# A typed graph layer: bf16 thirds of x replaced by two float32r parts, and a count matrix built and multiplied in two halves

## The chip, the cores and the metric

One Trainium2 chip, one core used. The metric is the device time of one launch in microseconds (us); lower is better. TensorE (PE) multiplies matrices into PSUM, VectorE (DVE) and ScalarE (ACT) work on tensors in SBUF and PSUM, GpSimd (POOL) here issues the indirect transfers that gather rows, SyncE (SP) issues most other transfers.

## The reference, cut to what matters

```python
N, E, D = 12500, 400000, 128            # nodes, edges (sorted by dst), features
def layer(X, src, dst, edge_types, W_data, b_data, W_control, b_control, W_self, b_self):
    Xs = X[src]
    m_data = Xs @ W_data.T + b_data
    m_ctrl = Xs @ W_control.T + b_control
    msg = where((edge_types == 0)[:, None], m_data, m_ctrl)
    agg = segment_sum(msg, dst, num_segments=N)
    return relu(agg + (X @ W_self.T + b_self))
result = layernorm(x + layer(x, ...))   # over the last axis, eps 1e-5, all float32
```

Since the weights come after a sum, the kernel first sums the x rows of each node's incoming edges, once for each of the two edge types, and multiplies the two sums by the two weights afterwards.

## The kernel before, in words

The nodes are split in two parts that are worked on at the same time.

**By matrix (dense blocks).** The first 88 x 64 = 5632 destination nodes are taken in blocks of 64 nodes. For a block the kernel needs a matrix of counts: for each source node (98 chunks of 128) and each of 128 columns (64 nodes x 2 types) how many edges there are. The edges of a node are looked at as up to 64 keys. A *batch* is 8 columns' worth of work in each half of the partitions: VectorE writes one-hot matrices `hot_p` (source node within its chunk) and `hot_q` (chunk and type) by comparing tables with keys (`make_onehots`, L1126), TensorE multiplies them (`build`, L634: 8 matmuls of 196 columns, in two PSUM buffers z = 0 and 1), and ScalarE moves each buffer into `cnt` (`evacuate`, L848, two copies of 784 elements). The one-hots of two groups of 64 partitions are multiplied in different row halves of the array. Eight batches make a block. Then `apply` (L652) multiplies the block's counts by x: 98 matmuls accumulated in `apply_ps`, with one 128x128 chunk of `cnt` as the stationary operand and the matching chunk of `x3` as the moving one. `x3` holds x as three bf16 parts side by side and a column of ones, 385 columns, so that the bf16 products add up to the exact float32 sum. VectorE adds up the three parts (`post`), TensorE turns the result, ScalarE takes it to `fin`.

**By gather.** The edges from tile 1395 on (tiles of 128 edges) are taken in 173 rounds of 10 tiles. For each tile GpSimd issues an indirect transfer of 128 rows into `rows`. A matmul with a one-hot matrix of 64 columns (`hot`, made by `make_hot`) adds them up in `sum_ps` (`gather_sums`, L616; even and odd tiles write different halves of the PSUM partitions). The first 12 rounds gather float32 rows of x, and ScalarE takes the sums (`take_sums`). All later rounds gather bf16 rows of 768 bytes from `x3_dram`, which ScalarE's queue wrote at the start, and VectorE adds up the parts (`add_parts`, L1188). A moving window of sums in `acc` is updated by `add_sums`.

**Order.** The whole program is a list of steps written out by the same Python loop for each engine. In step s TensorE does, in this order: `gather_sums` if a round starts here, `build(s)`, the step's one job in the PSUM tile `misc` (transposes, products with the weights), then one eighth of `apply` (12 or 13 matmuls). The apply of a block runs 8 steps behind its build; `cnt` has two buffers, one per block. There are 88 x 8 = 704 batches and so some 712 steps. A gather round starts every fourth step (a few places are left out), and GpSimd's ten transfers of a round wait at three places for `built` (`QUARTER`, L45), so that they spread over four steps.

The handshake that matters below: `build(n)` writes buffer z only when ScalarE has emptied it of batch n-1:

```python
                    if j >= 2:
                        pe.wait_ge(evacuated, j - 1)
...
                for z in range(2):
                    act.wait_ge(built, 2 * n + z + 1)
```

Before the steps, x is loaded in 14 chunks and split (`split_hi` and `split_mid` on ScalarE, `split_rest` and `split_low` on VectorE). The keys are written to DRAM in 11 pieces from which GpSimd gathers each block's keys.

Of the kernel before, what the change touches and what calls it, by code (L numbers as in the profile page):

```python
# [8 lines left out]
F32 = mybir.dt.float32  # L9
BF16 = mybir.dt.bfloat16  # L10
# [6 lines left out]
P = 128  # L17
D = 128
GT = 5
WIN = 32  # L20
TYPE_STEP = 16384
# [4 lines left out]
BLOCKS = 88  # L26
DENSE = BLOCK * BLOCKS
GATHER_0 = 1395
# [5 lines left out]
KEY_TILES = 1441  # L34
EW = 64
SLOTS = 20
F32_ROUNDS = 12
ROW = 3 * D
AHEAD = 2
BUILD_AT = 0  # L40
APPLY_AT = BUILD_AT + 8
XB = 7
FIRST_X = 5
DKCH = 11
# [5 lines left out]
def gnn_resnorm(nc, x, src, dst, etype, w_data, b_data, w_ctrl, b_ctrl, w_self, b_self, out):  # L50
# [8 lines left out]
    XBLOCKS = -(-N // P)  # L59
    XCH = XBLOCKS // XB  # L60
# [4 lines left out]
    assert KEY_TILES % DKCH == 0 and SLOTS == AHEAD * 2 * GT  # L65

    places = (BATCHES + APPLY_AT) // 4 - (0 if BLOCKS == 86 else 1)
    spare = places - PAIRS
    left_out = {2 * ((places * (2 * i + 1) // (2 * spare)) // 2) + 1 for i in range(spare)}
    gather_step = [4 * j for j in range(places) if j not in left_out][:PAIRS]  # L70
    assert len(gather_step) == PAIRS
# [95 lines left out]
    with ctx:  # L167
        def sb(name, shape, dt=F32):
            return ctx.enter_context(nc.sbuf_tensor(name, shape, dt))

        def sem(name):
            return ctx.enter_context(nc.semaphore(name))
# [6 lines left out]
        x3_dram = nc.dram_tensor("x3_dram", [N, ROW], BF16).ap()  # L179
# [11 lines left out]
        key_t = sb("key_t", [P, GROUPS * GT])  # L191
        off_i = sb("off_i", [1, GROUPS], I32)
# [27 lines left out]
        out_sb = sb("out_sb", [P, 2, D])  # L220
# [7 lines left out]
        key_ok = sb("key_ok", [P, 2, EW])  # L228
# [14 lines left out]
        xs = [cnt[:, 1, 14 * i:14 * i + 14, :].rearrange("p b c -> p (b c)").bitcast(F32) for i in range(3)]  # L243
# [12 lines left out]
        def region(b0, nb, dt):  # L256
            return x3[:, b0:b0 + nb, :].rearrange("p b c -> p (b c)").bitcast(dt)
# [1135 lines left out]
```

## Time and profile before

| | us |
|---|---|
| median of 3 runs | 2812.58 (2806.29 to 2814.47) |
| the profiled execution, its own time | 2784.88 |
| its span, first to last instruction | 2783.0 |
| TensorE busy with matmuls | 2364.6 (85%) |
| GpSimd / VectorE / ScalarE busy | 1691.7 / 1266.1 / 1224.5 |

"Busy" counts the time in which at least one instruction of that kind runs. A matmul's duration contains the time to drain the array, so consecutive matmuls overlap: their spacing, not their duration, is what a stream costs. The granted TensorE clock was 0.96 of full speed on average.

### The profile page before, as it was taken

How to read it: one execution, taken by the hardware profiler on the slowest of the kernel's cores; microseconds unless marked ns; L12 is line 12 of the kernel's file. 1: busy time of each engine (PE TensorE's matmuls, PEld its weight loads, DVE VectorE, ACT ScalarE, POOL GpSimd, SP SyncE). 2: the span in 40 equal slices, each digit the busy share in tenths (PEclk: the TensorE clock that was granted, in tenths of full speed). 3: DMA queues.
4: the chain of work that ended last, by engine and by line, in shares of the span. 5: the costliest groups of instructions: out<-in, count | busy, mean ns of one | idle time of the engine just before them, and what ended most of it. 6: DMA issues, size and time to landing. Idle time of an engine off the chain costs nothing.

```text
span 2783.0 us, 47819 instructions
## 1 busy us (share of the span) xinstructions
PE 2364.6 (85%) x17776; PEld 1301.3 (47%) x17776; DVE 1266.1 (45%) x4037; ACT 1224.5 (44%) x1997; POOL 1691.7 (61%) x1785
## 2 busy tenths in 40 slices
PE   3688888888888888888889888988888888888988
PEld 2344444544444444444445454444444444444444
DVE  8444444445444444444444454444444444444443
ACT  6344444444444444444444444444444444444443
POOL 6466665666666665666666666566666666656662
PEclk9899999999999999999999999999999999999999
DMA  7712222222222222222222222222222222222221
GB/s 191 223 47 67 71 72 59 73 68 74 72 73 71 73 72 62 74 69 75 71 72 73 69 75 71 63 69 73 74 69 73 71 73 72 69 61 72 71 75 34
DMA packets 150380, 211.42 MB, mean 76 GB/s; under 512 B 35298, under 2 KB 120725, under 8 KB 150147
## 3 DMA queue, kind: packets, MB, share of 16 engines
q0 software_dynamic: 83232, 170.57, 22.0%
q1 hardware_dynamic: 54177, 28.15, 3.7%
q10 hardware_dynamic: 12738, 9.60, 1.1%
q8 instruction: 145, 2.38, 0.3%
q14 instruction: 88, 0.72, 0.1%
HBM read 189.78 MB, written 18.41 MB: 75 GB/s over the span
## 4 chain that ended last, share of the span: by engine, by line
PE 44%; another core or an unknown queue 23%; ACT 14%; DVE 9%; issue 7%; DVEq 2%; DMA 1%; SPq 0%; ACTq 0%
PE apply_ps L664 25%; ACT cnt L860 13%; PE build L648 8%; PE sum_ps L630 4%; DVEq L1177 2%; DVE hot_q L1136 2%; DVE hot_p L1136 1%; PE misc L673 1%; DVE acc L1183 1%; PE misc L714 1%; DVE sg L1193 1%; PE misc L717 1%; DMA key_dram<-fin 1%; PE misc L692 1%
## 5 line engine op out<-in xcount | busy, mean ns | idle before, releaser
L560 POOL DMA_INDIRECT rows<-x_dram,src_t x1610 | 1524.7, 947 | 947.5 <-issue 383.4
L860 ACT ACTIVATE cnt<-build 128x784 bf16<-128x784 f32 x1408 | 1087.5, 822 | 1457.1 <-remote 773.1
L664 PE MATMUL apply_ps<-x,cnt 128*128 128x385 bf16 x8624 | 1611.2, 337 | 31.0 <-issue 25.5
L664 PEld LDWEIGHTS apply_ps<-x,cnt 128*128 128x128 bf16 x8624 | 868.3, 103 | 604.7 <-issue 135.7
L648 PE MATMUL build<-hot_q,hot_p 64*128 64x196 bf16 x5632 | 425.1, 254 | 274.2 <-ACT cnt L860 205.6
L648 PEld LDWEIGHTS build<-hot_q,hot_p 64*128 64x128 bf16 x5632 | 197.6, 95 | 572.7 <-issue 372.7
L1136 DVE TENSOR_TENSOR hot_q<-const_ps,key_pq 128x784 bf16<-128x784 bf16 x704 | 390.3, 554 | 0.0
L1181 DVE TENSOR_TENSOR acc_deg<-misc,acc_deg 2x32 f32 x346 | 61.9, 179 | 671.2 <-remote 278.7
L1136 DVE TENSOR_TENSOR hot_p<-const_ps,key_pq 128x512 bf16<-128x512 bf16 x704 | 291.2, 414 | 43.1 <-DVE acc L1183 16.5
L560 POOL DMA_INDIRECT rows<-in_x,src_t x120 | 122.8, 1024 | 76.8 <-issue 30.5
L1191 DVE TENSOR_TENSOR zg<-t_mask,sum_ps 128x2 f16<-128x2 f32 x161 | 24.9, 154 | 307.5 <-PE sum_ps L630 158.3
L630 PE MATMUL sum_ps<-rows,hot 128*64 128x385 bf16 x1610 | 162.5, 331 | 0.0
L1216 DVE SCALAR_TENSOR_TENSOR y_sb<-misc,x_u 128x128 f32<-128x128 f32 (+3 forms) x105 | 30.4, 290 | 268.1 <-PE misc L717 163.9
L1041 DVE TENSOR_TENSOR hot<-const_ps,key_t 128x640 bf16<-128x640 f32 (+1 forms) x173 | 140.9, 814 | 0.0
L630 PEld LDWEIGHTS sum_ps<-rows,hot 128*64 128x64 bf16 x1610 | 77.1, 108 | 76.7 <-issue 52.1
L1193 DVE TENSOR_REDUCE sg<-sum_ps 128x128 f32<-128x384 f32 x161 | 88.7, 551 | 0.0
L1183 DVE TENSOR_TENSOR acc<-misc,acc 128x64 f32 x346 | 77.7, 225 | 2.1 <-issue 2.1
L1210 DVE TENSOR_TENSOR zd<-t_mask,apply_ps 128x2 f16<-128x2 f32 x88 | 13.6, 155 | 127.2 <-remote 45.6
L673 PE MATMUL misc<-ident,sg 128*128 128x128 f32 x173 | 58.8, 340 | 0.0
L692 PE MATMUL misc<-ident,x_u 128*128 128x128 f32 (+3 forms) x105 | 35.0, 333 | 27.1 <-DVEq L1186 14.3
L672 PE MATMUL misc<-picks,zg 128*2 128x64 f16 x173 | 33.2, 192 | 25.9 <-DVEq L1099 19.4
L537 POOL DMA_INDIRECT key_raw<-key_dram,key_at x44 | 41.8, 949 | 21.5 <-issue 13.1
(182 smaller groups left out, 1082.5 us busy)
## 6 DMA issues: line engine op xcount, KB each, us to landing
rows<-x_dram,src_t POOLq DMA_INDIRECT x1610
x_dram<-x ACTq DMA_DIRECT2D x13, 672.0 KB
cnt<-in_x SPq DMA_DIRECT2D x13, 448.0 KB
x_u<-in_x SPq DMA_DIRECT2D x43, 64.0 KB
out<-out_sb SPq DMA_DIRECT2D x43, 64.0 KB
key_dram<-fin SPq DMA_DIRECT2D x12, 196.5 KB
x_u<-in_x SPq DMA_DIRECT2D x40, 53.5 KB
out<-out_sb SPq DMA_DIRECT2D x40, 53.5 KB
```

Source lines behind the costliest of these rows:

```text
L560: pool.indirect_dma_start(out=rows_f[:, slot, 0:D] if early else rows[:, slot, 0:ROW], out_offset=None, in_=x if early else x3_dram, in_of ...
L630: last = pe.matmul(sum_ps[part, 0:ROW + 1], hot_b[:, ps % 3, st, :], rows[:, slot, 0:ROW + 1], start=(j == 0), stop=(j == GT - 1))
L648: last = pe.matmul(build_ps[z][:, o:o + 2 * XBLOCKS], hot_p[half, slot, :, i], hot_q[half, slot, :, i], start=True, stop=True)
L664: last = pe.matmul(apply_ps[:, 0:385], cnt[:, k % 2, b, :], x3[:, b, 0:385], start=(b == 0), stop=(b == XBLOCKS - 1))
L673: pe.transpose(misc[:, 0:P], sg[:, ps % 2, 0:D], ident[:, :]).then_inc(misc_full, 1)
L692: pe.transpose(misc[:, 0:v.r], x_u[0:v.r, i % 3, :], ident[0:v.r, 0:v.r]).then_inc(misc_full, 1)
L860: act.activation(o, i.rearrange("p h (m b) -> p b h m", b=XBLOCKS), ACT.Copy).then_inc(evacuated, 1)
L1041: dve.tensor_tensor(to[:, ps % 3, :, :], const_ps[:, HOT].unsqueeze(1).to_broadcast([P, 2 * GT, 2 * WIN]), keys.unsqueeze(2).to_broadcast( ...
L1136: last = dve.tensor_tensor(to[:, z:z + 2, :, :], table.unsqueeze(1).to_broadcast([P, 2, w, 2]), keys.unsqueeze(2).to_broadcast([P, 2, w, 2 ...
L1181: dve.tensor_tensor(dw, misc[0:2, P + 32 * g:P + 32 * g + 32], dw, ALU.add)
L1183: dve.tensor_tensor(aw, misc[:, 64 * g:64 * g + 64].rearrange("p (t w) -> p t w", t=2), aw, ALU.add).then_inc(acc_step, 1)
L1193: dve.tensor_reduce(sg[:, ps % 2, 0:D], sum_ps[:, 0:ROW].rearrange("p (k d) -> p d k", k=3), AX.X, ALU.add).then_inc(sg_ready, 1)
```

## The change

1. **x in two parts.** `x2` holds x as two float32r parts (a high part and the rest) and two columns of ones, 258 columns. The moving operand and `cnt` both become float32r. The split needs one ScalarE pass and one VectorE pass per chunk in place of two and two. `post` adds two parts.
2. **Two halves of source blocks.** `cnt` has two buffers of 49 chunks each (a half, in 4 bytes an element) in place of two of 98 (in 2 bytes). A batch now covers 16 columns in each half of the partitions for 49 of the 98 chunks: `build` is 16 matmuls of 98 columns. Four batches make a half, eight a block as before. `hot_p` is made once per two halves (1024 elements every other group of four batches), `hot_q` keeps 784 elements a batch. `evacuate` still moves 2 x 784 elements, now as float32r.
3. **Apply** runs by halves, 4 steps behind, in portions of 6, 12, 12, 12 and 7 matmuls; the last 7 stand at the start of the step in which the next half begins.
4. **98 blocks by matrix** instead of 88: 784 batches, 9604 apply matmuls; 157 gather rounds in place of 173, one every 5.02 steps.
5. **All gathers are float32** rows of 512 bytes from x itself, with float32 matmuls of 129 columns. `x3_dram`, its writes and `add_parts` are gone; ScalarE's `take_sums` (two short instructions) serves all rounds.
6. Smaller: `key_t` and the comparison table in bf16 with the type as a half step, `hot` in two buffers, `hot_q` for three batches instead of four, dense keys in 15 pieces, outputs normalised in place (`out_sb` is gone), loads of x without waiting for the split up to chunk 6, small tensors put over other ones.

```diff
-BLOCKS = 88
+BLOCKS = 98
-GATHER_0 = 1395
+GATHER_0 = 1555
-ROW = 3 * D
+ROW = 2 * D
-APPLY_AT = BUILD_AT + 8
+APPLY_AT = BUILD_AT + 4
+PORTIONS = (6, 12, 12, 12, 7)
-DKCH = 11
+DKCH = 15
...
+    gather_step = [(BATCHES + APPLY_AT) * r // PAIRS for r in range(PAIRS)]
...
-        x3 = sb("x3", [P, XBLOCKS, 386], BF16)
-        cnt = sb("cnt", [P, 2, XBLOCKS, P], BF16)
+        x2 = sb("x2", [P, XBLOCKS, ROW + 2], F32R)
+        cnt = sb("cnt", [P, 2, HALF, P], F32R)
-        rows = sb("rows", [P, SLOTS, ROW + 2], BF16)
-        hot = sb("hot", [P, 3, 2 * GT, 2 * WIN])
-        hot_p = sb("hot_p", [P, 8, P, 2], BF16)
-        hot_q = sb("hot_q", [P, 8, 2 * XBLOCKS, 2], BF16)
+        rows = sb("rows", [P, SLOTS, D + 1])
+        hot = sb("hot", [P, 2, 2 * GT, 2 * WIN])
+        hot_p = sb("hot_p", [P, 16, P, 2], BF16)
+        hot_q = sb("hot_q", [P, 12, 2 * HALF, 2], BF16)
...
             def build(n):
...
-                    for i in range(2):
-                        slot = (2 * n + z) % 8
+                    for j in range(4 * z, 4 * z + 4):
+                        pair, r = divmod(j, 2)
                         for h in range(2):
-                            half = slice(64 * h, 64 * h + 64)
-                            o = WIDE * h + 2 * XBLOCKS * i
-                            last = pe.matmul(build_ps[z][:, o:o + 2 * XBLOCKS], hot_p[half, slot, :, i],
-                                             hot_q[half, slot, :, i], start=True, stop=True)
+                            part = slice(64 * h, 64 * h + 64)
+                            o = WIDE * h + 2 * HALF * (j % 4)
+                            last = pe.matmul(build_ps[z][:, o:o + 2 * HALF], hot_p[part, 4 * q4 + pair, :, r],
+                                             hot_q[part, 4 * (n % 3) + pair, :, r], start=True, stop=True)
                     last.then_inc(built, 1)
...
-                for b in range(b0, b1):
-                    last = pe.matmul(apply_ps[:, 0:385], cnt[:, k % 2, b, :], x3[:, b, 0:385],
+                for i in range(b0, b1):
+                    b = half * HALF + i
+                    last = pe.matmul(apply_ps[:, 0:ROW + 2], cnt[:, half, i, :], x2[:, b, :],
                                      start=(b == 0), stop=(b == XBLOCKS - 1))
...
             for s in range(STEPS):
+                y, c = divmod(s - APPLY_AT, 4)
+                if c == 0 and 0 < y <= 2 * BLOCKS:
+                    apply(y - 1, 4)
                 if s in gather_at:
                     gather_sums(gather_at[s])
                 if batch_at(s) is not None:
                     build(batch_at(s))
...
-                if F32_ROUNDS <= gather_at.get(s, 0):
-                    add_parts(gather_at[s])
...
-                if gather_at.get(s, PAIRS) < F32_ROUNDS:
+                if s in gather_at:
                     take_sums(gather_at[s])
...
                 for z in range(2):
                     act.wait_ge(built, 2 * n + z + 1)
-                    c0 = 8 * (2 * (n % 8) + z)
-                    o = cnt[:, k % 2, :, c0:c0 + 8].rearrange("p b (h m) -> p b h m", h=2)
-                    i = build_ps[z][:, :].rearrange("p (h c) -> p h c", h=2)[:, :, 0:4 * XBLOCKS]
-                    act.activation(o, i.rearrange("p h (m b) -> p b h m", b=XBLOCKS), ACT.Copy
+                    c0 = 32 * q4 + 16 * z
+                    o = cnt[:, y % 2, :, c0:c0 + 16].rearrange("p b (h m) -> p b h m", h=2)
+                    i = build_ps[z][:, :].rearrange("p (h c) -> p h c", h=2)[:, :, 0:8 * HALF]
+                    act.activation(o, i.rearrange("p h (m b) -> p b h m", b=HALF), ACT.Copy
                                    ).then_inc(evacuated, 1)
```

How the rows stand on TensorE in the steady part, first in the kernel before, four steps that contain one gather round (L630). Each row is a run of equal instructions, its output tile, its inputs, the output's shape and the count:

```order
L673 MATMUL misc<-ident,sg 128x128
L664 MATMUL apply_ps<-x,cnt 128x385 x12
L648 MATMUL build<-hot_q,hot_p 128x196 x8
L678 MATMUL misc<-picks,zd 2x64
L679 MATMUL misc<-ident,sd 128x128
L664 MATMUL apply_ps<-x,cnt 128x385 x12
L648 MATMUL build<-hot_q,hot_p 128x196 x8
L692 MATMUL misc<-ident,x_u 128x106
L664 MATMUL apply_ps<-x,cnt 128x385 x13
L630 MATMUL sum_ps<-rows,hot 64x385 x10
L648 MATMUL build<-hot_q,hot_p 128x196 x8
```

The same engine in the changed kernel (L638 is `build`, L656 `apply`, L620 `gather_sums`):

```order
L665 MATMUL misc<-ident,sg 128x128
L656 MATMUL apply_ps<-x,cnt 128x258 x12
L638 MATMUL build<-hot_q,hot_p 128x98 x16
L670 MATMUL misc<-picks,zd 2x64
L671 MATMUL misc<-ident,sd 128x128
L656 MATMUL apply_ps<-x,cnt 128x258 x19
L638 MATMUL build<-hot_q,hot_p 128x98 x16
L656 MATMUL apply_ps<-x,cnt 128x258 x6
L638 MATMUL build<-hot_q,hot_p 128x98 x16
L656 MATMUL apply_ps<-x,cnt 128x258 x12
L620 MATMUL sum_ps<-rows,hot 64x129 x10
```

Between two builds there were always 12 or 13 apply matmuls; now there are 12, 12, 19 (12 and the 7 left over) and 6 in turn. Each float32 matmul of L620 is written here once, and shows as two instructions in a trace.

On ScalarE, a stretch of the changed kernel (L833 is `evacuate`, L816 and L818 `take_sums`, L862 the normalising, L850 and L856 the copy of x and the square root):

```order
L856 ACTIVATE std<-mv,eps_t 128x1
L816 ACTIVATE sg<-sum_ps 128x129
L818 ACTIVATE zg<-t_mask,sg 128x2
L833 ACTIVATE cnt<-build 128x49x16 x4
L856 ACTIVATE std<-mv,eps_t 107x1
L862 ACTIVATE y_sb<-y_sb,shift,rstd 128x128
L833 ACTIVATE cnt<-build 128x49x16 x2
```

The pair L816 and L818 stands ahead of the two copies of its step, in every round; before, it stood there in the first 12 rounds alone, and VectorE did that work in the others.

## Rows read from the trace of the kernel before

**Rows 1.** The page: TensorE's busy time, and its granted clock in 40 slices.
```profile
PE 2364.6 (85%) x17776; PEld 1301.3 (47%) x17776; DVE 1266.1 (45%) x4037; ACT 1224.5 (44%) x1997; POOL 1691.7 (61%) x1785
PEclk9899999999999999999999999999999999999999
```

**Rows 2.** Busy time of each engine by stretch, the start and one steady stretch.
```profile
core 0: us, PE busy (x) PEld busy (x) DVE busy (x) ACT busy (x) POOL busy (x), PEclk, DMA share, GB/s
0.00:40.00 40.00, 12.14 (x67) 9.68 (x67) 31.90 (x101) 18.68 (x27) 23.99 (x29) 1.00 0.86 226
40.00:100.00 60.00, 27.45 (x197) 14.65 (x199) 41.70 (x111) 33.42 (x48) 35.82 (x35) 0.89 0.75 225
1200.00:1600.00 400.00, 349.36 (x2597) 189.91 (x2598) 179.58 (x573) 175.55 (x285) 253.66 (x268) 0.95 0.26 72
```

**Rows 3.** The page's costliest groups: count, busy us, mean ns, idle before.
```profile
L560 POOL DMA_INDIRECT rows<-x_dram,src_t x1610 | 1524.7, 947 | 947.5 <-issue 383.4
L860 ACT ACTIVATE cnt<-build 128x784 bf16<-128x784 f32 x1408 | 1087.5, 822 | 1457.1 <-remote 773.1
L664 PE MATMUL apply_ps<-x,cnt 128*128 128x385 bf16 x8624 | 1611.2, 337 | 31.0 <-issue 25.5
L648 PE MATMUL build<-hot_q,hot_p 64*128 64x196 bf16 x5632 | 425.1, 254 | 274.2 <-ACT cnt L860 205.6
L1136 DVE TENSOR_TENSOR hot_q<-const_ps,key_pq 128x784 bf16<-128x784 bf16 x704 | 390.3, 554 | 0.0
L1136 DVE TENSOR_TENSOR hot_p<-const_ps,key_pq 128x512 bf16<-128x512 bf16 x704 | 291.2, 414 | 43.1 <-DVE acc L1183 16.5
```

**Rows 4.** Groups by shape, window 0 to 150: the builds done by then.
```profile
L648 PE MATMUL build<-hot_q,hot_p 64*128 64x196 bf16 x185 | 17.6, 294 | 34.5 <-ACT cnt L860 21.9 <-DVE hot_q L1136 7.3 <-issue 4.3
```

**Rows 5.** Timeline: a stretch of 12 apply matmuls, and one of 49.
```profile
1402.19 2.14 PE L664 MATMUL apply_ps<-x,cnt 128*128 128x385 bf16 x12
...
2761.21 8.25 PE L664 MATMUL apply_ps<-x,cnt 128*128 128x385 bf16 x49
```

**Rows 6.** Timeline: float32 products with the weights, back to back.
```profile
1405.04 0.39 PE L715 MATMUL misc<-w_t,fin 128*128 128x128 f32 x2
...
1405.27 0.39 PE L716 MATMUL misc<-w_t,fin 128*128 128x128 f32 x2
```

**Rows 7.** Timeline: a float32 gather round and a bf16 one on TensorE.
```profile
138.29 1.32 PE L627 MATMUL sum_ps<-rows,hot 128*64 128x129 f32 x20
...
1407.95 1.01 PE L630 MATMUL sum_ps<-rows,hot 128*64 128x385 bf16 x10
```

**Rows 8.** Timeline: half a batch of build, and two whole ones.
```profile
1400.14 0.35 PE L648 MATMUL build<-hot_q,hot_p 64*128 64x196 bf16 x4
...
1387.22 0.53 PE L648 MATMUL build<-hot_q,hot_p 64*128 64x196 bf16 x8
...
1404.26 0.52 PE L648 MATMUL build<-hot_q,hot_p 64*128 64x196 bf16 x8
```

**Rows 9.** Timeline: ScalarE's copies of the two whole batches of rows 8.
```profile
1387.62 0.82 ACT L860 ACTIVATE cnt<-build 128x784 bf16<-128x784 f32 x1 [0.90 <-issue]
...
1407.39 1.54 ACT L860 ACTIVATE cnt<-build 128x784 bf16<-128x784 f32 x2 [4.08 <-remote]
```

**Rows 10.** Timeline: two consecutive gathers on GpSimd.
```profile
1402.67 0.94 POOL L560 DMA_INDIRECT rows<-x_dram,src_t  x1 [0.30 <-issue]
...
1403.92 0.95 POOL L560 DMA_INDIRECT rows<-x_dram,src_t  x1 [0.31 <-issue]
```

**Rows 11.** Timeline: ScalarE's part of an early float32 round.
```profile
141.62 0.28 ACT L843 ACTIVATE sg<-sum_ps 128x129 f32<-128x129 f32 x1 [4.26 <-remote]
141.94 0.29 ACT L845 ACTIVATE zg<-t_mask,sg 128x2 f16<-128x2 f32 x1
```

**Rows 12.** Groups by shape, window 0 to 150: a copy that writes float32 with a stride.
```profile
L803 ACT ACTIVATE key_t<-build 128x512 f32<-128x512 f32 x2 | 2.2, 1124 | 0.0
```

**Rows 13.** The lines of build: durations ns min/median/max, first and last start us.
```profile
L648 PE MATMUL build<-hot_q,hot_p x5632: 243/246/364, 37.4 to 2746.4; 64*128 64x196 bf16 x195
```

More of the change, by code:

```diff
@@ L9 @@
 F32 = mybir.dt.float32
+F32R = mybir.dt.float32r
 BF16 = mybir.dt.bfloat16
@@ L20 @@
 WIN = 32
-TYPE_STEP = 16384
 EPS = 1e-5
@@ L64, in gnn_resnorm @@
     assert (TILES - GATHER_0) % (2 * GT) == 0 and BLOCKS % 2 == 0 and XBLOCKS % XB == 0 and DENSE > WIN_0
[L65 to L71, printed above, removed]
+    assert KEY_TILES % DKCH == 0 and SLOTS == AHEAD * 2 * GT and sum(PORTIONS) == HALF
+    gather_step = [(BATCHES + APPLY_AT) * r // PAIRS for r in range(PAIRS)]
     taken = set()
@@ L169, in sb, with under @@
             return ctx.enter_context(nc.sbuf_tensor(name, shape, dt))
+        def under(name, shape):
+            with nc.sbuf_tensor(name, shape, F32) as t:
+                return t
         def sem(name):
@@ L463, in _ @@
                     load_dkeys(c + 2)
+            sp.wait_ge(dkeys_written, 16 * (DKCH + 1))
+            for i in range(3):
+                load_unit(i, units[i].n0, units[i].r)
             for s in range(STEPS):
@@ L625, in gather_sums @@
                     part, st = slice(64 * g, 64 * g + 64), g * GT + j
-                    if ps < F32_ROUNDS:
-                        last = pe.matmul(sum_ps[part, 0:D + 1], hot[:, ps % 3, st, :], rows_f[:, slot, 0:D + 1],
-                                         start=(j == 0), stop=(j == GT - 1))
-                    else:
-                        last = pe.matmul(sum_ps[part, 0:ROW + 1], hot_b[:, ps % 3, st, :], rows[:, slot, 0:ROW + 1],
-                                         start=(j == 0), stop=(j == GT - 1))
+                    last = pe.matmul(sum_ps[part, 0:D + 1], hot[:, ps % 2, st, :], rows[:, slot, 0:D + 1],
+                                     start=(j == 0), stop=(j == GT - 1))
@@ L1126, in make_onehots @@
             def make_onehots(n):
[L1128 to L1130 removed]
+                k, half, q4 = n // 8, n // 4 % 2, n % 4
+                g, q = n // 32, 32 * (k % 4) + 8 * q4
+                if n >= 3:
+                    dve.wait_ge(built, 2 * (n - 2))
                 if n % 32 == 0:
                     dve.wait_ge(misc_free, key_job(g) + 1)
[L1133 to L1138 removed]
@@ L1139, in make_onehots @@
-                last.then_inc(onehot_ready, 1)
-            def split_rest(c):
+                keys_p, keys_q = (key_pq[:, g % 2, i, q:q + 8].rearrange("p (j r) -> p j r", r=2) for i in range(2))
+                if half == 0:
+                    dve.tensor_tensor(
+                        hot_p[:, 4 * q4:4 * q4 + 4, :, :], table_p.unsqueeze(1).to_broadcast([P, 4, P, 2]),
+                        keys_p.unsqueeze(2).to_broadcast([P, 4, P, 2]), ALU.is_equal)
+                z = 4 * (n % 3)
+                dve.tensor_tensor(
+                    hot_q[:, z:z + 4, :, :],
+                    table_q[:, half, :, :].unsqueeze(1).to_broadcast([P, 4, 2 * HALF, 2]),
+                    keys_q.unsqueeze(2).to_broadcast([P, 4, 2 * HALF, 2]), ALU.is_equal).then_inc(onehot_ready, 1)
```

303 lines of the change are left out of this document (116 added, 187 removed).

## The prediction

> **What bounds the kernel now.** I read the page first: TensorE is busy 2364.6 of 2783.0 us, GpSimd 61%, the two others under half [rows 1]. The table by stretch says that this is even: in 1200 to 1600 TensorE works 349.36 of 400 us at a clock of 0.95 [rows 2]. The builds run from 37.4 to 2746.4 [rows 13]: 704 steps at 3.85 us. So the span is a start of some 37 us, the steps, and a tail of 37 us, and a step is TensorE's own work (2364.6 / 704 = 3.36 us) plus its idle time. The groups say what that work is: apply 1611.2 us busy, build 425.1, the rest small; and the named wait is build's on ScalarE's copies, 205.6 us [rows 3]. ScalarE itself is idle 1457 us before those copies, over half of it for releases that the trace does not name. The timeline shows why: a batch built at 1387.22 is taken up by ScalarE at 1387.62, but one built at 1404.26 only at 1407.39, though ScalarE had nothing else to do [rows 8, 9]. TensorE's completions arrive sometimes at once and sometimes 1 to 3 us late. Each step is thus a race: TensorE's apply and odd jobs on one side, and on the other this delay plus two copies (1.54 us) and the way back. Usually TensorE is the longer side.
>
> **The change part by part**, in the profiled execution's own time.
>
> *Apply.* 49 matmuls take 8.25 us and 12 take 2.14 [rows 5], so a 385-column one costs (8.25 - 2.14) / 37 = 0.165 us. All: 8624 x 0.165 = 1423 us. A float32r product with 258 columns is not in the trace. The nearest row is float32: one product with 128 columns is two instructions, and the next product begins 0.23 us later [rows 6], some 0.11 us an instruction. Against the bf16 spacing (0.165 / 385 = 0.43 ns a column), 0.11 us is 256 columns, so each of the two instructions streams its 128 columns twice. That gives both ends: one pass over 258 columns is 0.110 us, two passes 0.220. The same rows show that a 128-column float32 weight load hides under a 0.11 us stream. I take one pass: 9604 x 0.110 = 1056 us, that is -367. The trace has no row with one pass over 4-byte data, so this is the largest unknown. The Trainium skill's page "FP8 and Floating Point Precision", section "TensorE Precision Notes", says that true FP32 takes four passes and that a reduced-precision read cuts a 4-byte value to FP22, which would be the one-pass case; its page on reading traces ("Perfetto Trace Analysis", the footnote on what 100% means) halves the rate for FP32_LOW_HIGH, which would make it 2113 us. Apply's stretches become more (784 for 704), each with 2.14 - 12 x 0.165 = 0.16 us of drain: +13.
>
> *Build.* Half a batch takes 0.35 us and a whole one 0.52 to 0.53 [rows 8], so two pairs of 196-column matmuls (two row halves run together) cost 0.17, or 0.087 a pair. Columns in total are the same, 16 x 98 for 8 x 196. If a pair goes by its columns, a batch costs as before, 0.604 us (425.1 / 704); 80 more batches: +48. If a pair cannot be shorter than 0.087, it is 8 x 0.087 instead of 4: +0.35 us a step. I take the first, since the 20 instructions of a float32 round go through in 1.32 us, 10 pairs of 0.11, so short pairs are at least possible.
>
> *Gathers.* A float32 round takes 1.32 us, a bf16 one 1.01 [rows 7]. Before: 161 x 1.01 + 12 x 1.32 = 178; now 157 x 1.32 = 207: +29.
>
> *Odd jobs.* Ten more block turns and three more key turns against sixteen fewer round turns: 0.
>
> *ScalarE.* 1568 copies of 822 ns are 1289 us [rows 3], and a round costs it 0.28 + 0.29 us [rows 11]: 157 x 0.57 = 89. Its load stays near 1.9 us a step, hidden behind TensorE's. Writing 4 bytes is the open point: a float32 copy with a stride of 20 bytes took 1124 ns for 512 elements [rows 12], 2.2 ns each against 1.05. Here 16 elements lie side by side, so I take 822 ns; the other end is 1.7 us a copy.
>
> *VectorE.* hot_p now has 1024 elements every other batch: from 554 and 414 ns for 784 and 512 elements [rows 3] it comes to 0.68 us, 0.89 us of one-hots a step for 0.97 before. It loses `add_parts`. Hidden. With one buffer of one-hots fewer it still works two batches ahead.
>
> *GpSimd.* Gathers follow each other at 1.25 us [rows 10]. 1570 and 50 for keys are 2025 us, below the forecast span. If rows of 512 bytes cost what those of 768 did, it does not bind; it is the floor, some 2090 us.
>
> *Start.* By 150 us there were 185 / 8 = 23 batches [rows 4]; at the steady pace it would have been 29, so the start costs some 20 us beyond the 37. The split of x goes from four passes to two and fewer loads wait for it; but the second half of `cnt` is still the staging place, and dense keys take longer to write. I take back most of it: -20.
>
> *Sum.* TensorE busy: 2364.6 - 367 + 13 + 48 + 29 = 2088 us. Idle before: 2783.0 - 2364.6 = 418, of which 60 lie in the first 100 us [rows 2] and 358 in the steps, 0.51 us each. At the same idle time a step: 2088 + 784 x 0.51 + 60 - 20 = 2528 us. The profiled execution's own time is 2 us above its span and 28 us (1.0%) under the median of the runs, so this is 2530 x 1.01 = 2555 us. A step would last 3.16 us in place of 3.85.
>
> **The rivals.**
>
> *A. As summed:* 2450 to 2680 us. Chance 0.52.
>
> *B. The handshake takes what apply gives.* TensorE's side of the race falls by 0.7 us a step (3.36 to 2.66), ScalarE's does not, and after the portion of 6 matmuls (0.66 us) TensorE is back at build long before two copies are done; `take_sums` now stands ahead of them too. If a quarter to a half of the steps lose all of the 0.7: +137 to +274, which is 2690 to 2830 us. For it: the 3.1 us in [rows 8, 9], which no portion covers. Against: the portions of 12 and 19 with the odd jobs still outlast 1.6 us when the signal is prompt. Chance 0.17.
>
> *C. Idle shrinks with the work.* If waits are a share of the work (358 / 2305 = 15.5%), the span is 60 - 20 + 2048 x 1.155 = 2405, so 2430 us, and less (to 2370) if completions come promptly more often, now that GpSimd's ten gathers are spread over five steps and not four. Chance 0.18.
>
> *D. Slower: short matmuls do not get cheaper.* A pair of 98 columns costs the 0.087 us of 196: +0.35 x 784 = +274, 2830 us. It decides from 0.078 us a pair: then the gain of 257 us is gone. For it: nothing in the trace streams for long at less than 0.11 us a pair, and instructions on TensorE rise from 35,552 to some 54,000. Against: what is seen goes by columns. 196 columns cost 0.087, 385 cost 0.165, so 0.41 ns each and 0.006 us fixed, with no floor in sight down to 196; for 98 the line gives 0.046 us. Chance 0.06. The Trainium skill bears on it: "TensorE: Matmul & The Clock Gate", section "Wait — 56ns, not 53.3ns?", puts the cost of a matmul at 62 ns when the sequencer decodes it in its own code, whatever its columns. By that rule a batch of 16 would need 0.99 us, which would be +0.56 a step, 2995 us; with decoding in hardware it gives a floor of 25 ns instead, and no loss.
>
> *E. Slower: float32r takes two passes.* Apply costs 9604 x 0.220 = 2113: +690 instead of -367, about 3610 us. Chance 0.07.
>
> **How the numbers follow.** The measurement of this kernel can tell 0.3% from no change, 2804 to 2821. Faster: A 0.52, C 0.18, and 0.12 of B, together 0.82. Within: 0.02 of B and 0.01 of D. Slower: 0.03 of B, 0.05 of D, E. The range for 8 in 10 reaches from the low end of C to the upper part of B, 2370 to 2800 us; the likeliest is 2555.
>
> **What would show it.** Right: in a stretch of 12 apply matmuls the row reads about 1.5 us; a batch of build still 0.5; steps of 3.0 to 3.3 us; TensorE busy near 2090; GpSimd's spacing 1.25. Wrong: a stretch of 12 at 2.8 us (E); a batch of build at 0.85 (D); the wait of build on ScalarE's copies well over 400 us (B) or copies well above 822 ns. The kernel would be faster than I say if TensorE's idle time in the steps fell below 300 us.

## The result, and the profile after

| | us |
|---|---|
| changed kernel, median of 4 runs | 2909.72 (2900.31 to 2912.53) |
| kernel before, on the same chip | 2810.97 (2806.29 to 2814.47) |
| ratio | 1.0347, 95% interval 1.0333 to 1.0362 |
| predicted | 2555 (2370 to 2800) |

The changed kernel is 3.5% slower here; I had said 9% faster. The page of its profiled run (2900.31 us), the rows that answer to [rows 1] and [rows 3]:

```profile
span 2898.4 us, 65825 instructions
...
PE 2354.4 (81%) x26955; PEld 2021.5 (70%) x26955; DVE 1203.5 (42%) x3465; ACT 1431.9 (49%) x2452; POOL 1541.2 (53%) x1632
...
PEclk8799989999999989899999999999999999998999
...
L833 ACT ACTIVATE cnt<-build 128x784 fp32r<-128x784 f32 x1568 | 1234.2, 821 | 1212.9 <-PE build L638 598.4
L656 PE MATMUL apply_ps<-x,cnt 128*128 128x258 f32 x9604 | 1466.2, 303 | 140.9 <-issue 71.2
L638 PE MATMUL build<-hot_q,hot_p 64*128 64x98 bf16 x12544 | 515.0, 214 | 258.5 <-ACT cnt L833 158.7
...
L620 PE MATMUL sum_ps<-rows,hot 128*64 128x129 f32 x3140 | 256.3, 309 | 22.7 <-issue 21.8
```

TensorE's work hardly fell, from 2364.6 to 2354.4 us where 2088 was forecast, and its idle time rose from 418 to 544. The term-by-term miss against the forecast span of 2528:

| term | forecast | measured | difference |
|---|---|---|---|
| apply (1611.2 - 367 + 13) | 1257 | 1466.2 | +209 |
| build (425.1 + 48) | 473 | 515.0 | +42 |
| gathers (178 + 29) | 207 | 256.3 | +49 |
| other TensorE work | 151 | 116.9 | -34 |
| TensorE idle | 440 | 544.0 | +104 |

The timeline of the same kernel, stretches from four places (start, duration; TensorE's apply in portions of 12, 19 and 6, a build, and ScalarE's copies of it):

```profile
1207.41 2.93 PE L656 MATMUL apply_ps<-x,cnt 128*128 128x258 f32 x12
...
1406.54 0.55 PE L638 MATMUL build<-hot_q,hot_p 64*128 64x98 bf16 x16
...
1407.23 1.69 PE L656 MATMUL apply_ps<-x,cnt 128*128 128x258 f32 x12
...
1408.35 1.54 ACT L833 ACTIVATE cnt<-build 128x784 fp32r<-128x784 f32 x2 [3.67 <-PE build L638]
...
1409.32 0.37 PE L638 MATMUL build<-hot_q,hot_p 64*128 64x98 bf16 x8 [0.40 <-issue]
...
1409.94 0.21 PEld L638 LDWEIGHTS build<-hot_q,hot_p 64*128 64x128 bf16 x8 [0.41 <-ACT cnt L833]
...
2864.30 2.53 PE L656 MATMUL apply_ps<-x,cnt 128*128 128x258 f32 x19
...
2868.14 0.96 PE L656 MATMUL apply_ps<-x,cnt 128*128 128x258 f32 x6
```

Three things are to be seen. Twelve apply matmuls take 1.69 us, not 1.5, even when nothing disturbs them (granted clock 1.00 from 1407.23 to 1408.92). At other places the same twelve take 2.93: there the granted clock is 0.50, its lower level of 1.2 GHz. And the batch built at 1406.54 is taken up by ScalarE only at 1408.35, some 1.5 us after its first eight matmuls, as it was before [rows 9]; TensorE then stands still until 1409.32 and its next batch comes in two pieces.

The waits, TensorE's and then ScalarE's (us in all, times, longest):

```profile
PE build L638 <- ACT cnt L833: 158.7, 271, 6.5
PE build L638 <- issue: 86.3, 130, 6.7
PE apply_ps L656 <- issue: 71.2, 107, 3.2
PE apply_ps L656 <- DVE sd L1153: 68.4, 50, 4.8
PE misc L676 <- DVE key_n L1083: 25.7, 13, 3.2
...
ACT cnt L833 <- remote: 587.9, 213, 9.6
```

So the wait that rival B named did not grow: 158.7 us against 205.6 before. Some of the waits called "issue" belong to it: the one at 1409.32 ends 0.15 us after ScalarE's first copy. But all idle time ahead of build together is 258.5 us against 274.2 before [rows 3]. What grew is the idle time ahead of apply (31.0 to 140.9 us) and of the gather sums (none to 22.7): waits named "issue", and one for VectorE's reading of `apply_ps` (`sd`, 68.4 us).

The stretch 1200 to 1600 answers to [rows 2]: TensorE busy 333 of 400 us at a clock of 0.93, before 349 at 0.95.

```profile
1200.00:1600.00 400.00, 333.01 (x3857) 286.19 (x3853) 165.54 (x475) 201.96 (x348) 218.12 (x231) 0.93 0.16 45
```

The mean clock is 0.923 for 0.960 before. A mean of c means a share of 2(1 - c) at half clock: 446 us of this span, 223 us of the one before.

### The profile page after: what moved, and what is told of

It is laid out like the page before. It is cut to its first block, busy times and chain, and to the rows that moved or that the text cites. A ratio compares the mean times of both kernels' runs of the same rounds, so it can differ in the third digit from the quotient of the medians.

```text
span 2898.4 us, 65825 instructions
## 1 busy us (share of the span) xinstructions
PE 2354.4 (81%) x26955; PEld 2021.5 (70%) x26955; DVE 1203.5 (42%) x3465; ACT 1431.9 (49%) x2452; POOL 1541.2 (53%) x1632
## 4 chain that ended last, share of the span: by engine, by line
PE 55%; another core or an unknown queue 14%; ACT 11%; issue 8%; DVE 6%; DVEq 3%; SPq 1%; DMA 1%; ACTq 0%
PE apply_ps L656 27%; PE build L638 13%; ACT cnt L833 10%; PE sum_ps L620 7%; DVEq L1127 3%; DVE hot_q L1100 2%; PE misc L665 2%; PE misc L706 1%; DVE acc L1133 1%; PE misc L709 1%; PE misc L707 1%; PE misc L708 1%; PE misc L671 1%; DVE hot_p L1096 1%
## 5 line engine op out<-in xcount | busy, mean ns | idle before, releaser
L555 POOL DMA_INDIRECT rows<-in_x,src_t x1570 | 1490.6, 949 | 1279.0 <-PE sum_ps L620 527.8
L833 ACT ACTIVATE cnt<-build 128x784 fp32r<-128x784 f32 x1568 | 1234.2, 821 | 1212.9 <-PE build L638 598.4
L656 PE MATMUL apply_ps<-x,cnt 128*128 128x258 f32 x9604 | 1466.2, 303 | 140.9 <-issue 71.2
L656 PEld LDWEIGHTS apply_ps<-x,cnt 128*128 128x128 f32 x9604 | 1315.3, 204 | 191.1 <-issue 164.1
L638 PE MATMUL build<-hot_q,hot_p 64*128 64x98 bf16 x12544 | 515.0, 214 | 258.5 <-ACT cnt L833 158.7
L638 PEld LDWEIGHTS build<-hot_q,hot_p 64*128 64x128 bf16 x12544 | 342.3, 98 | 435.3 <-issue 185.9
L1096 DVE TENSOR_TENSOR hot_p<-const_ps,key_pq 128x1024 bf16<-128x1024 bf16 x392 | 269.3, 687 | 355.6 <-remote 174.8
L1131 DVE TENSOR_TENSOR acc_deg<-misc,acc_deg 2x32 f32 x314 | 56.3, 179 | 552.1 <-remote 284.5
L620 PE MATMUL sum_ps<-rows,hot 128*64 128x129 f32 x3140 | 256.3, 309 | 22.7 <-issue 21.8
L620 PEld LDWEIGHTS sum_ps<-rows,hot 128*64 128x64 f32 x3140 | 204.1, 154 | 59.9 <-issue 42.6
L816 ACT ACTIVATE sg<-sum_ps 128x129 f32<-128x129 f32 x157 | 43.8, 279 | 190.8 <-PE sum_ps L620 178.1
L1001 DVE TENSOR_TENSOR hot<-const_ps,key_t 128x640 f32<-128x640 f32 x157 | 127.6, 813 | 0.0
L862 ACT ACTIVATE y_sb<-y_sb,shift,rstd 128x128 f32<-128x128 f32 (+3 forms) x104 | 50.8, 488 | 2.8 <-DVE shift L1171 2.8
L665 PE MATMUL misc<-ident,sg 128*128 128x128 f32 x157 | 51.8, 330 | 0.0
L818 ACT ACTIVATE zg<-t_mask,sg 128x2 f16<-128x2 f32 x157 | 46.5, 296 | 5.1
```

Source lines behind the costliest of these rows:

```text
L555: pool.indirect_dma_start(out=rows[:, slot, 0:D], out_offset=None, in_=x, in_offset=bass.IndirectOffsetOnAxis(ap=src_t[:, col:col + 1], ax ...
L620: last = pe.matmul(sum_ps[part, 0:D + 1], hot[:, ps % 2, st, :], rows[:, slot, 0:D + 1], start=(j == 0), stop=(j == GT - 1))
L638: last = pe.matmul(build_ps[z][:, o:o + 2 * HALF], hot_p[part, 4 * q4 + pair, :, r], hot_q[part, 4 * (n % 3) + pair, :, r], start=True, st ...
L656: last = pe.matmul(apply_ps[:, 0:ROW + 2], cnt[:, half, i, :], x2[:, b, :], start=(b == 0), stop=(b == XBLOCKS - 1))
L665: pe.transpose(misc[:, 0:P], sg[:, ps % 2, 0:D], ident[:, :]).then_inc(misc_full, 1)
L833: act.activation(o, i.rearrange("p h (m b) -> p b h m", b=HALF), ACT.Copy).then_inc(evacuated, 1)
```

## The experiments

The twelve ran on three chips, numbered 3 (`a1` to `b1`), 0 (`c0` to `c3`) and 7 (`d0` to `d3`), and the kernel before took 2313.99, 2313.49 and 2315.15 us there instead of 2811. As these agree within 0.1%, runs are compared across the three, which are called the faster chips below. The chip of the result, whose number isn't known, is called the first chip; that it is another one is taken from its time and its late take-ups. Each ratio is to the kernel before on the same chip. The difference between 2811 and 2313 became a subject of its own.

### 1. What an apply matmul costs: element type and columns

`a1_bf16_two_parts`: the change with x in two bf16 parts and `cnt` in bf16; it leaves out the third part of x.

```diff
-        x2 = sb("x2", [P, XBLOCKS, ROW + 2], F32R)
+        x2 = x2_raw[:, :, :].bitcast(BF16)[:, :, 0:ROW + 2]
-        cnt = sb("cnt", [P, 2, HALF, P], F32R)
+        cnt = cnt_raw[:, :, :, :].bitcast(BF16)[:, :, :, 0:P]
```

> The changed kernel, with x2 and cnt in bf16 instead of float32r and everything else as it is: the same 9604 apply matmuls of 258 columns, the same steps (it leaves out the third part of x, so it computes with x cut to 16 bits of mantissa). Theory W (float32r's weight load sets the pace of apply): the spacing in apply falls from 0.121 us to 0.110, the late second matmul of each stretch goes, so a stretch of 12 reads 1.5 us in place of 1.69; that is 9604 x 0.011 + 784 x 0.08 = 168 us less work, time 2909 - 168 = 2740, or down to 2680 with the small delays that float32r shows inside a stretch. Rival T (twice as much time at the half clock and the handshake make the loss, not the load): a stretch still shows 1.5 us, but time stays above 2850 because waits take what is freed.

Measured: 2180.36 us, ratio 0.9419 (0.9403 to 0.9435). Its row of apply, and three stretches:

```profile
L656 PE MATMUL apply_ps<-x_raw,cnt_raw 128*128 128x258 bf16 x9604 | 1205.3, 275 | 22.7 <-DVE sd L1153 20.7
L656 PEld LDWEIGHTS apply_ps<-x_raw,cnt_raw 128*128 128x128 bf16 x9604 | 933.9, 100 | 169.5 <-issue 23.7
...
2102.39 1.50 PE L656 MATMUL apply_ps<-x_raw,cnt_raw 128*128 128x258 bf16 x12
...
2104.52 0.33 PE L665 MATMUL misc<-ident,sg 128*128 128x128 f32 x1
2104.68 2.25 PE L656 MATMUL apply_ps<-x_raw,cnt_raw 128*128 128x258 bf16 x19
2106.87 0.55 PE L638 MATMUL build<-hot_q,hot_p 64*128 64x98 bf16 x16
...
2108.17 0.82 PE L656 MATMUL apply_ps<-x_raw,cnt_raw 128*128 128x258 bf16 x6 [0.49 <-ACT cnt_raw L833]
```

(2.25 - 0.82) / 13 = 0.110 us a matmul and 0.16 a stretch: exactly the forecast's figures, but for bf16.

The unaltered change, on another of the faster chips (`c0_after_again`, experiment 3), has this in the same place:

```profile
1413.30 0.33 PE L665 MATMUL misc<-ident,sg 128*128 128x128 f32 x1
1413.38 2.52 PE L656 MATMUL apply_ps<-x,cnt 128*128 128x258 f32 x19
1415.84 0.55 PE L638 MATMUL build<-hot_q,hot_p 64*128 64x98 bf16 x16
```

From the transpose (L665) to the next build, 19 matmuls take 2.54 us in float32r and 2.35 in bf16, that is 19 x 0.010. The float32r row looks longer by 0.27 us because it starts earlier, 0.08 us behind the transpose's start and not 0.16. That start is overlap with the work ahead of it and costs no time.

`a2_130_columns`: the change with float32r, moving only 130 of the 258 columns; it leaves out the high part of x.

```diff
-                    last = pe.matmul(apply_ps[:, 0:ROW + 2], cnt[:, half, i, :], x2[:, b, :],
+                    last = pe.matmul(apply_ps[:, D:ROW + 2], cnt[:, half, i, :], x2[:, b, D:ROW + 2],
```

> The changed kernel with apply streaming only columns 128 to 257 of x2 (130 columns, still float32r; it leaves out the high part of x). Theory W: the spacing stays near 0.12 us, since the 128-column weight load is as long as before, and the time moves by under 2%. Rival N (columns set the pace, with a fixed 0.012 us on top): the spacing falls to 0.066 us, a stretch of 12 to 1.0 us, and the time by 300 us or more. A third way: float32r is slow under 256 columns, then the spacing rises to 0.2 us.

Measured: 2293.49 us, ratio 0.9911 (0.9878 to 0.9944).

```profile
PEclk9799999999999989797999998999996798999899
...
2101.11 1.56 PE L656 MATMUL apply_ps<-x,cnt 128*128 128x130 f32 x12
...
2106.56 2.32 PE L656 MATMUL apply_ps<-x,cnt 128*128 128x130 f32 x19
...
2109.50 0.86 PE L656 MATMUL apply_ps<-x,cnt 128*128 128x130 f32 x6
```

(2.32 - 0.86) / 13 = 0.112 us with half the columns, where the unaltered change has (2.53 - 0.96) / 13 = 0.121. What remains when the columns go is the load of 128 columns of 4-byte counts: the rows of the loads themselves (PEld) have a mean of 194 ns with 4-byte counts and 100 ns with bf16. No run took few columns with bf16 counts, so the load as the cause rests on these rows. The third way, float32r slow at few columns, is out. The kernel as a whole got 25 us slower than the unaltered change (below, 2268): its clock was 0.923 for 0.982, and gathers and build, whose work is the same, rose from 212.4 to 234.0 and from 452.5 to 474.0 us. Why the clock fell is open.

`a3_386_columns`: 386 columns moved, the next chunk's first part beside each chunk, which adds numbers that are of no use to the sum.

```diff
+                    wide = ROW + 2 + (D if b < XBLOCKS - 1 else 0)
-                    last = pe.matmul(apply_ps[:, 0:ROW + 2], cnt[:, half, i, :], x2[:, b, :],
+                    last = pe.matmul(apply_ps[:, 0:wide], cnt[:, half, i, :], x2_flat[:, (ROW + 2) * b:(ROW + 2) * b + wide],
```

> The changed kernel with 386 columns in each apply matmul (128 more, whose results nobody reads). Column-bound by any theory: spacing 0.161 to 0.165 us, stretch of 12 at 2.15 us, TensorE's work up by 9604 x 0.042 = 400 us. Theory K (the half clock comes because TensorE has less to do per step): its share of time at the half clock falls back from 15% to 8%, granted clock 0.95 or more, and the time rises by less than 300 us, to about 3150. Without K: clock stays at 0.92 and the time rises by 400 us or more.

Measured: 2716.14 us, ratio 1.1738 (1.1714 to 1.1761).

```profile
2105.89 3.54 PE L658 MATMUL apply_ps<-x,cnt 128*128 128x386 f32 x19
...
2111.09 1.34 PE L658 MATMUL apply_ps<-x,cnt 128*128 128x386 f32 x6
```

(3.54 - 1.34) / 13 = 0.169 us; over all apply matmuls of this trace the median spacing is 0.177, a little over the 0.161 to 0.165 expected. Of the two expectations neither came whole: the clock is 0.992, as theory K had it, and the time rose by 448 us over the unaltered change, as the case without K had it; on the faster chips little time at the lower clock was left to win back. So one float32r matmul costs 0.112, 0.121 and 0.169 us at 130, 258 and 386 columns: one pass, on a floor of 0.11 that the weight load seems to set, and at 258 columns, where both sides cost about 0.11, neither hides wholly under the other.

### 2. The gathers alone

`b1_float32_gathers`: the kernel before with all 173 rounds float32, and `take_sums` on ScalarE for all.

```diff
-F32_ROUNDS = 12
+F32_ROUNDS = 173
-                if ps == F32_ROUNDS:
+                if ps == 12:
```

> The kernel before with one part of the change: all 173 rounds gather float32 rows of x and ScalarE's take_sums serves them in place of add_parts (the bf16 copy of x is still written). By the sum it costs 161 x 0.31 = 50 us of TensorE's time: 2810 + 50 = 2860. If take_sums on ScalarE ahead of the copies matters for the handshake: 100 us or more, 2910. If VectorE's relief helps more than that costs: below 2830.

Measured: 2349.93 us, ratio 1.0156 (1.0139 to 1.0173): +36 us for 161 rounds, 0.22 each. The forecast had 0.31 each on TensorE, where the trace has 0.27: the rounds take 232.1 us for 188.7. So the gathers' part of the change costs what it should, and `take_sums` ahead of the copies costs nothing to be seen here, where the answers are prompt.

### 3. The changed kernel on the faster chips

`c0_after_again`: the changed kernel, unaltered. `d0_before_again`: the kernel before, unaltered, for its trace.

> The changed kernel once more, unaltered, beside the kernel before on this call's chip. On the chip of the first four experiments the kernel before took 2314 us where it took 2811 for the verdict, and TensorE's completions there reached the other engines at once. Theory L (late completions carry most of the waits, and the loss is float32r's): where they are prompt the waits nearly vanish from both kernels, before is at 2314 and the changed one at 2330 to 2400, ratio 1.01 to 1.04. Rival H (the loss came only from waits that late completions cause): with prompt completions the changed kernel is faster than before, below 2280.

Measured: 2268.09 us (2264.56 to 2269.24) against 2313.49, ratio 0.9798 (0.9781 to 0.9814). Here the same kernel is 2% faster. That is under the 2280 of rival H and not the 2330 to 2400 of my theory L: with prompt answers float32r's cost alone doesn't turn the change into a loss.

> The kernel before, unaltered, for a trace on the chip that these runs get. If this is a chip on which ScalarE takes a batch up at once (the second chip so far: changed kernel 2268, before 2313), build waits 20 to 60 us for ScalarE in all, TensorE is busy 2240 to 2275 us (97%), and an apply stretch of 12 takes 2.0 to 2.15 us, most of them near 2.05. If late signals belong to the kernel before and not to the chip, the wait of build on ScalarE's copies reads near 200 us here too, and the trace shows idle time of 400 us.

Measured: 2313.92 us, ratio 0.9995 (0.9986 to 1.0005). Build's wait is 21.0 us, so late signals do not come with this kernel by itself. The pages, first of the changed kernel:

```profile
PE 2112.7 (93%) x26955; PEld 1867.9 (82%) x26955; DVE 1196.5 (53%) x3465; ACT 1405.9 (62%) x2452; POOL 1538.9 (68%) x1632
...
L656 PE MATMUL apply_ps<-x,cnt 128*128 128x258 f32 x9604 | 1367.6, 292 | 18.1 <-DVE sd L1153 16.7
L656 PEld LDWEIGHTS apply_ps<-x,cnt 128*128 128x128 f32 x9604 | 1236.0, 194 | 43.9 <-issue 21.6
...
L638 PE MATMUL build<-hot_q,hot_p 64*128 64x98 bf16 x12544 | 452.5, 208 | 30.9 <-ACT cnt L833 22.8
...
L620 PE MATMUL sum_ps<-rows,hot 128*64 128x129 f32 x3140 | 212.4, 280 | 3.4 <-DMA rows<-in_x,src_t 3.4
```

and of the kernel before:

```profile
span 2309.5 us, 47819 instructions
...
PE 2223.8 (96%) x17776; PEld 1286.4 (56%) x17776; DVE 1274.0 (55%) x4037; ACT 1227.6 (53%) x1997; POOL 1688.9 (73%) x1785
...
L664 PE MATMUL apply_ps<-x,cnt 128*128 128x385 bf16 x8624 | 1544.0, 328 | 3.4 <-DVE sd L1211 3.4
...
L648 PE MATMUL build<-hot_q,hot_p 64*128 64x196 bf16 x5632 | 373.1, 250 | 25.6 <-ACT cnt L860 21.0
```

The same terms on the faster chips, as changes: apply -176 (forecast -354), build +79 (+48), all gathers +24 (+29; before they are 168.6 and 20.1), the rest of TensorE's work -38 (0), idle +69 (+21, from 85.7 to 154.6): -42 in all, where the forecast had -255. The -38 is not less work: the rest is 118.0 us before, 80.2 in the change and 122.2 in the bf16 version with the same odd jobs, so it is the overlap of experiment 1 and belongs to apply, which then is -214. The waits of TensorE, the changed kernel's and then two of the kernel before:

```profile
PE misc L676 <- DVE key_n L1083: 36.9, 20, 3.2
...
PE build L638 <- ACT cnt L833: 22.8, 52, 3.6
PE apply_ps L656 <- DVE sd L1153: 16.7, 30, 9.3
PE misc L670 <- DVEq L1136: 11.6, 36, 1.4
```

```profile
PE build L648 <- ACT cnt L860: 21.0, 8, 4.6
...
PE misc L684 <- DVE key_n L1123: 1.2, 1, 1.2
```

VectorE, which I had called hidden, now keeps TensorE waiting where keys are turned and where `apply_ps` or the sums are taken. And ScalarE's waits show how the chips differ: no row "remote" for its copies here, in either kernel, where the first chip has 587.9 us over 213 waits (773.1 over 220 before). Waits so named, for a release that the profile can't place, stand on the first chip before VectorE's and GpSimd's work too (`acc_deg` 284.5 us, `rows` 135.5), and nowhere in these two traces. The timeline of the changed kernel on a faster chip:

```profile
1402.18 0.55 PE L638 MATMUL build<-hot_q,hot_p 64*128 64x98 bf16 x16
...
1402.58 1.54 ACT L833 ACTIVATE cnt<-build 128x784 fp32r<-128x784 f32 x2 [0.78 <-PE build L638]
```

A batch built at 1402.18 is taken up 0.40 us later, as soon as its first half is there. Counted over the whole traces: where ScalarE is idle when a half is finished, its copy begins 0.04 us later here, never more than 0.05, in both kernels (601 and 364 cases); on the first chip the median is 1.5 us before and 1.3 in the change, and the longest 5.8 and 6.2 (377 and 204 cases).

### 4. Even portions; and a bf16 version of fewer blocks

`c1_even_portions`: 12, 12, 15 and 10 apply matmuls between builds instead of 12, 12, 19 and 6.

```diff
-PORTIONS = (6, 12, 12, 12, 7)
+PORTIONS = (10, 12, 12, 12, 3)
```

> The changed kernel with portions 10, 12, 12, 12, 3 of apply instead of 6, 12, 12, 12, 7, so that at least 10 apply matmuls lie between any two builds. Theory B (after the portion of 6 TensorE is back at build before ScalarE's two copies are done, and waits): the wait of build on ScalarE's copies falls and the time by 0.4 us x 196 = 80 us, 3%. Rival: the short portion is covered by the odd jobs and the next step's slack; then the time moves by less than 0.5%.

Measured: 2240.84 us, ratio 0.9682 (0.9665 to 0.9698), 27 us below the unaltered change, 1.2%, which lies between the 80 us of theory B and the rival's 0.5%. Build's wait for ScalarE falls from 22.8 to 10.1 us and build itself from 452.5 to 437.9: a batch whose second half waits costs more also in busy time (two pieces of 0.36 for one of 0.55). By the traces 103 of the 784 batches come in two pieces in the unaltered change and 20 with the even portions.

`c2_a1_again` is the bf16 version once more.

> The kernel of a1_bf16_two_parts beside the changed kernel on one chip. Theory W: faster than c0_after_again by 168 us or more (0.011 us of spacing on 9604 matmuls, 0.08 us at the start of 784 stretches). Rival T: by less than 60 us.

Measured: 2179.77 us, ratio 0.9421 (0.9402 to 0.944), 88 us below the unaltered change on the same chip. Both expectations missed: theory W had 168 or more, rival T less than 60. Apply's row falls by 165 us (1367.6 to 1202.5), but TensorE's busy time only by 118 (2112.7 to 1995.1), since the 0.08 us a stretch was overlap, and 30 us come back as idle time (154.6 to 184.7).

`c3_bf16_94_blocks`: the bf16 version (without the third part of x) with 94 blocks by matrix and more by gather, `cnt` packed.

```diff
-BLOCKS = 98
+BLOCKS = 94
-GATHER_0 = 1555
+GATHER_0 = 1495
```

> Two bf16 parts as in a1_bf16_two_parts, and 94 blocks by matrix with 163 gather rounds instead of 98 with 157 (it leaves out the third part of x). In a1 TensorE was busy 92% and GpSimd had slack (71%), a step took 2.7 us: 32 steps fewer is -86 us, 6 rounds more on TensorE +8. GpSimd's floor is 1630 + 48 transfers x 1.25 = 2100 us plus 40. If TensorE sets the pace: 2180 - 78 = 2100 to 2120, against 2314 before on a chip with prompt completions; if GpSimd does: 2150 to 2170.

Measured: 2159.91 us, ratio 0.9335 (0.932 to 0.9351), the fastest of all, and 0.9% below the 98 blocks. TensorE's busy time falls from 1999.9 to 1963.5 us; its wait for gathered rows, 3.4 us in the unaltered change, is 30.7 here, so this direction is nearly used up: the time lies in the 2150 to 2170 expected if GpSimd sets the pace, and not in the 2100 to 2120 if TensorE does.

### 5. A late handshake, made on purpose

The faster chips answer promptly, so lateness can be added. In every third batch ScalarE's first copy is done three times; both PSUM buffers come free some 1.7 us later. Nothing else differs. `d1_before_held` and `d2_after_held` have this edit, `d3_even_held` has it and the even portions.

```diff
+                    held = 2 if z == 0 and n % 3 == 0 else 0
...
+                    for c in range(held):
+                        act.activation(o, i.rearrange("p h (m b) -> p b h m", b=HALF), ACT.Copy
+                                       ).then_inc(held_copy, 1)
+                        act.wait_ge(held_copy, 2 * (n // 3) + c + 1)
```

> The kernel before, in which ScalarE's first copy of every third batch is done three times, so that both buffers come free 1.7 us later (235 of 704 steps). Theory 'race' (a step is the longer of TensorE's apply with its odd jobs and the handshake): of the 1.7 us the 12 apply matmuls and the job cover nearly all beyond what they cover already, 0.2 to 0.5 us is lost: +50 to +120 us, 2365 to 2435. Rival 'queue' (a hold costs what it lasts, as ScalarE's queue is tight anyway): 235 x 1.7 = +400, 2710. Rival 'clock' (the chip of the first comparison differs by its granted clock, not by the handshake): the hold costs the same in this kernel and the changed one.

Measured: 2429.53 us, ratio 1.0494 (1.0476 to 1.0512): +116, which is 0.49 us a held batch, as theory 'race' had it.

> The changed kernel with the same hold in every third batch (261 of 784). Theory 'race': after the portion of 6 nearly the whole 1.7 us is lost, after 12 about 1.0, after 19 about 0.2: mean 0.95 a held step, +250 (200 to 330), 2470 to 2600 us, and the kernel is slower than the held kernel before by 2 to 8%, where unheld it is 2% faster. The wait of build on ScalarE rises from 23 to 200 or more. Rival 'clock' or any cause that has nothing to do with the handshake: the hold adds no more than it adds to the kernel before, and the changed kernel stays 1 to 2% faster than it.

Measured: 2496.7 us, ratio 1.0782 (1.0764 to 1.08): +229, 0.87 us a held batch, again as 'race' had it (the unheld change, 2268.09, ran on another of the faster chips). So the changed kernel is 1.028 times the kernel before when both are held, and 0.980 when neither is: the same hold turns the sign.

> The changed kernel with apply portions of 10, 12, 12, 12 and 3 (so 12, 12, 15, 10 matmuls between builds in place of 12, 12, 19, 6) and the same hold. Theory 'race': the held step after the short portion loses 0.5 us less, the one after the long portion 0.5 us more at most: about the same wait or up to 65 x 0.5 = 30 us less, beside the 27 us that the even portions gave without a hold: 20 to 60 us under the held changed kernel. If the portion of 6 were the main cost under late signals, it would win over 100 us.

Measured: 2449.42 us, ratio 1.0587 (1.0569 to 1.0604): 47 us below the held change, within what was expected, and still 0.8% above the held kernel before. The short portion is a part of the cost, not most of it.

The busy row and the wait, of the held kernel before and then of the held change:

```profile
PE 2257.5 (93%) x17776; PEld 1279.0 (53%) x17776; DVE 1274.2 (52%) x4037; ACT 1595.9 (66%) x2467; POOL 1687.4 (69%) x1785
...
PE build L649 <- ACT cnt L866: 109.8, 310, 6.5
```

```profile
PE 2186.7 (87%) x26955; PEld 1910.0 (76%) x26955; DVE 1200.9 (48%) x3465; ACT 1815.0 (73%) x2976; POOL 1537.9 (61%) x1632
...
PE build L639 <- ACT cnt L839: 200.8, 371, 4.8
```

The hold adds 86 us of idle time and 34 of busy to the one, 162 and 74 to the other. The clock stays at 0.995 in the kernel before, for all its new idle time, and falls from 0.982 to 0.971 in the change (0.975 to 0.977 in its other runs).

## Why the prediction was wrong

The forecast span of 2528 us was missed by 370. The faster chips, where the change gave -42 us for the forecast -255, show 213 of them; the other 158 are on the first chip alone.

**Apply: right mechanism, wrong size (140 of the 213).** Float32r takes one pass, as taken; rival E is out. The page "FP8 and Floating Point Precision" of the Trainium skill, section "TensorE Precision Notes", says that true FP32 takes four passes and that a reduced-precision read cuts a 4-byte value to FP22. One pass for float32r is what I had read into it, and the trace bears that out: 0.121 us, not 0.220. But the step "the same rows show that a 128-column float32 weight load hides under a 0.11 us stream" failed. By experiment 1 a load of that kind costs about 0.11 us itself, so with 258 columns the two do not hide each other wholly: 0.121 for 0.110, or 9604 x 0.011 = 106 us. The bf16 version measures it for the kernel as a whole: TensorE's busy time is 113 and 118 us less in its two runs, and the run itself 88 us less. (Apply's own row differs by 162, 1367.6 - 1205.3, but part of that is overlap.) It is the largest single error that does not depend on the chip. The other 24 us are bf16's own: 1205.3 us where the forecast's figures give 1181. The row of [rows 6] had room for the error: 0.23 us for two is 0.115, which I rounded down.

**Build: right in the main (31 of the 213).** 98 columns cost half of 196: (0.55 - 0.37) / 4 = 0.045 us a pair, the 0.046 of the line in rival D, which is out. The 62 ns a matmul that the Trainium skill ("TensorE: Matmul & The Clock Gate", section "Wait — 56ns, not 53.3ns?") gives for decoding in the sequencer's own code are not what this trace shows: 16 matmuls take 0.55 us with their drain, at most 34 ns each. Of the 31 us that build costs above +48 on the faster chips, some 17 are the batches in two pieces (103 for 9 before, 0.18 us each); the rest is not assigned.

**Gathers: about right** on the faster chips (+24 for +29).

**"Hidden" VectorE: wrong (most of 47).** The forecast had +21 us of idle time, the faster chips show +69. Waits for `key_n` (36.9 us for 1.2), for `sd` (16.7 for 3.4) and behind VectorE's queue are most of it. The forecast kept the idle time a step, and had no term for VectorE. That a shorter step leaves these waits less cover is my reading; no run tested it by itself.

**The idle time of the first chip, and the clock: the step "at the same idle time a step" failed.** On the chip of the prediction both kernels meet late completions. Measured against the faster chips, they cost the kernel before 2783.0 - 2309.5 = 474 us, the change 2898.4 - 2267.3 = 631, if lateness is the whole of the difference. Of the 158 more, 57 are idle time and 101 busy time. The busy part is largely the clock, which was not in my sum at all: from the faster chips to the first, time at half clock rises by 200 us (0.995 to 0.960) in the kernel before and by 364 (0.982 to 0.923) in the change; work of half the speed over the 164 us more is worth up to 82. This is nearest to rival B in kind, since late answers took more than apply gave. But B's place was wrong: its sign, a wait of build on ScalarE's copies well over 400 us, never came, and the loss lies in many short waits and in the clock.

**Sums that were off without deciding anything.** Rival C left out the 40 us that TensorE works in the first 100 us [rows 2]: by its own rule it is 2445 and so about 2470 us, not 2430. In rival D the gain is gone from 0.085 us a pair, not 0.078; and 0.99 us for a batch against 4 x 0.087 is +0.64 a step, not +0.56.

**What was shown and what only argued.** Shown: the pace of float32r; that the sign of the change differs between the first chip and the faster ones; that the traces of the first have late take-ups in both kernels and the others have none; that a hold of 1.7 us in a third of the batches costs the change twice what it costs the kernel before, and turns 0.980 into 1.028. Argued: that the weight load is what sets float32r's floor, and that lateness is the whole of the difference between the chips. The held change waits 200.8 us for ScalarE where the first chip shows 158.7 and other waits beside it, so the hold copies the kind and not the pattern. What makes completions late there, and whether it is the chip or something else of that time, stays open, and so does what lowers the clock; no experiment ran there.

## What to carry to other kernels

Halving the columns of a matmul pays only down to the cost of its weight load, and that depends on the weights' type: read the load's own pace before giving both operands four bytes. A kernel whose TensorE waits on answers can lose more from late ones the shorter its stretches of independent work are: here 0.87 us a held batch against 0.49. It can lose a second time by the clock, as the change did and the held kernel before did not (0.995 with and without the hold). Where the measured chip shows late take-ups, cost a change for both cases, and take the shortest stretch between two handshakes, not the mean.

## What was not expected of the hardware

- The same kernel ran in 2811 us for the result and in 2313 to 2315 us on three chips afterwards. In the slower chip's trace ScalarE takes up a finished half batch 1.5 us late (built from 1406.54, copied from 1408.35), in the faster one's at once (1402.18 and 1402.58).
- The clock did not follow TensorE's busy share: with TensorE 93% busy it was 0.923 in the change with 130 columns, 0.982 in the unaltered change and 0.995 in the held kernel before; it was 0.992 with 386 columns (97% busy). What it follows stays open.
- ScalarE's copies cost the same 821 ns to float32r as to bf16, with 16 elements side by side.
